# A two-layer graph network on one core: segments that begin at other row blocks, a tail of 12 column blocks in two passes of six, 64-column matmul pairs, and VectorE scaling the last output groups

## The reference, cut to what matters

```python
def layer0(X, adj, W, b):
    deg = clip(sum(adj, axis=1) + 1.0, 1.0)
    h = (adj @ X + X) / deg
    z = relu(concat([X, h], 1) @ W + b)
    return z / max(norm(z, axis=1), 1e-12)
def layer1(features, adj, W):
    neigh = adj @ features / (sum(adj, axis=1) + 1.0)
    return concat([features, neigh], -1) @ W.T
x = layernorm(x + layer0(x, adj, W0, b0))
x = layernorm(x + layer1(x, adj, W1))
```

## Time and profile before

| | us |
|---|---|
| median of three runs | 778.35 |
| the profiled execution's own time | 778.61 |
| its span, first to last instruction | 776.7 |
| PE busy (matmuls) | 662.5 (85%) |
| DVE busy | 710.8 (92%) |
| ACT busy | 619.5 (80%) |
| POOL busy | 211.1 (27%) |

### The profile page before, as it was taken

How to read it: one execution, slowest core, us unless ns; L and a number is a source line. 1 busy time by engine, 2 the same in 40 slices (tenths; PEclk the granted TensorE clock), 3 DMA queues, 4 the chain that set the end, 5 groups by cost and what they waited for, 6 DMA issues and landing times.

```text
span 776.7 us, 28012 instructions
## 1 busy us (share of the span) xinstructions
PE 662.5 (85%) x11173; PEld 610.1 (79%) x11173; DVE 710.8 (92%) x2703; ACT 619.5 (80%) x848; POOL 211.1 (27%) x302
## 2 busy tenths in 40 slices
PE   1457777878788888989899999999999999999992
PEld 0357677878677787878798989989998989988992
DVE  4699988999999999999999999999999999988894
ACT  4879798999989898989898988887888988840037
POOL 2225433535333332424313030211102020201024
PEclk9978897989999999999999999999999999999997
DMA  9999999999999999999999999999999999800004
GB/s 302 386 420 420 416 410 420 420 419 419 417 420 421 402 420 404 418 416 415 413 402 418 381 420 372 400 360 408 381 398 386 395 383 387 349 2 3 3 21 93
DMA packets 46125, 274.55 MB, mean 353 GB/s; under 512 B 12647, under 2 KB 12711, under 8 KB 13223
## 3 DMA queue, kind: packets, MB, share of 16 engines
q1 hardware_dynamic: 45184, 270.55, 87.0%
q0 software_dynamic: 576, 2.10, 0.8%
q10 hardware_dynamic: 230, 0.07, 0.0%
HBM read 270.60 MB, written 2.10 MB: 351 GB/s over the span
## 4 chain that ended last, share of the span: by engine, by line
DVE 31%; PE 27%; DMA 12%; issue 12%; ACT 10%; POOL 7%; ACTq 0%; DVEq 0%; SPq 0%; POOLq 0%
PE s_ps L367 13%; DMA a_in<-in_adj 9%; DVE e L766 9%; ACT junk L557 7%; DVE t_sb L773 6%; POOL small L1119 6%; PE u_ps L385 4%; PE p_ps L353 3%; DMA xl<-in_x 3%; DVE q_sb L839 2%; DVE y_sb L833 2%; DVE u_sb L773 2%; DVE a_in L773 1%; PE z_ps L431 1%; PE p_ps L442 1%
## 5 line engine op out<-in xcount | busy, mean ns | idle before, releaser
L557 ACT ACTIVATE junk<-a_in 128x2048 uint8<-128x2048 uint16 x256 | 489.6, 1919 | 3.1 <-DMA a_in<-in_adj 3.0
L367 PE MATMUL s_ps<-xh,t_sb 128*128 128x129 f16 x4096 | 377.9, 247 | 22.9 <-DVE t_sb L773 20.2
L367 PEld LDWEIGHTS s_ps<-xh,t_sb 128*128 128x128 fp8e4 x4096 | 306.2, 100 | 50.5 <-DVE t_sb L773 24.7
L766 DVE TENSOR_SCALAR e<-a_in 128x2048 fp8e4<-128x2048 f32 x256 | 310.7, 1224 | 7.8 <-DMA a_in<-in_adj 6.9
L1127 POOL COPY store<-pk 128x32 uint32<-128x32 uint32 (+1 forms) x250 | 130.2, 562 | 312.0 <-ACT pk L566 312.0
L353 PE MATMUL p_ps<-pow_bf,e 128*128 128x16 bf16 x4096 | 141.8, 170 | 62.7 <-DVE e L766 58.9
L353 PEld LDWEIGHTS p_ps<-pow_bf,e 128*128 128x128 fp8e4 x4096 | 128.9, 96 | 79.2 <-DVE e L766 72.9
L773 DVE TENSOR_SCALAR t_sb<-pk 128x128 uint32<-128x128 uint32 x1024 | 150.8, 222 | 5.3 <-ACT pk L566 4.8
L1119 POOL TENSOR_TENSOR small<-small,minus_half 128x4 f32<-128x4 f32 x32 | 74.6, 2332 | 203.9 <-DVE small L827 162.5
L385 PE MATMUL u_ps<-xh,u_sb 128*128 128x128 f16 x1488 | 99.2, 218 | 0.0
L385 PEld LDWEIGHTS u_ps<-xh,u_sb 128*128 128x128 fp8e4 x1488 | 88.9, 97 | 1.2
(11 more groups left out here) (110 smaller groups left out, 486.9 us busy)
## 6 DMA issues: line engine op xcount, KB each, us to landing
a_in<-in_adj SPq DMA_DIRECT2D x256, 1024.0 KB, 10.3
xl<-in_x POOLq DMA_DIRECT2D x4, 512.0 KB, 16.1
out_h<-e SPq DMA_DIRECT2D x8, 256.0 KB, 2.6
b_sb<-in_L_gnn_b ACTq DMA_DIRECT2D x3, 0.2 KB
w_sb<-in_L_gnn_W ACTq DMA_DIRECT2D x1, 32.0 KB
w_raw<-in_L_gnn_W ACTq DMA_DIRECT2D x1, 32.0 KB
```

Of the source, the lines that this page charges most:

```text
L367: last = nc.tensor.matmul(s_ps[:, n % 2, at:GW], t_sb[:, b, :], xh[:, b, at:GW], start=(b == 0), stop=False)
L557: nc.scalar.activation(junk[:, t % 2, :], halves[t % R], ACT.Copy, scale=1.0 / 128, accum_out=half_sum[:, n, c:c + 1]).then_inc(s_half, 1)
L766: nc.vector.tensor_scalar(e8[:, c, :], a_in[:, t % R, :], 1.0, None, ALU.is_equal, saturate=False).then_inc(s_e, 1)
```

## The change

`START` becomes 0, 12, 20, 28, 32, 40, 48, 56. `low` is then 0, 8, 16, 24, 28, 36, 44, 52; the segment from 32 has a catch-up width of four blocks (24 to 27, done in slots 32 to 39) and the others eight. TAIL is 52, and the 12 blocks left go in two passes of six (`TW`).

The 64-column pairs: `catch_up`, and `tail_sums` in the second pass, multiply the high part and the low part by two matmuls of 64 columns that add up in the same 64 columns of PSUM, in place of one matmul of 128 columns. `add_piece`, and `add_tail` in the second pass, then add once and not twice.

Outputs: ACT scales groups 0 to 3, DVE scales groups 4 to 7 (`scale_rows`, one instruction for eight rows), and DVE makes the squares of the last group itself (`last_variance`). SyncE waits on a second semaphore for groups 4 to 7. The tail has eight unpack buffers instead of six.

```diff
-START = [0, 12, 20, 28, 36, 44, 52]
+START = [0, 12, 20, 28, 32, 40, 48, 56]
-VR = 6
+VR = 8
+NA = 4
+WIDTH = [low(s + 1) - low(s) for s in range(NQ - 1)] + [NB - TAIL]
+TW = WIDTH[-1] // 2
 # catch_up, PE
-                    for b in range(W):
-                        last = nc.tensor.matmul(u_rows[:, r, :], u_sb[:, r * W + b, :],
-                                                xh[:, low(q - 1) + b, 0:HP], start=(b == 0), stop=(b == W - 1))
+                    for b in range(w):
+                        for part in range(2):
+                            last = nc.tensor.matmul(u_rows[:, r, 0:F], u_sb[:, r * w + b, :],
+                                                    xh[:, low(q - 1) + b, part * F:(part + 1) * F],
+                                                    start=(b + part == 0), stop=(b + part == w))
 # add_piece, DVE
-                link(nc.vector.tensor_tensor(rows, u_rows[:, 0:r1 - r0, 0:F], rows, ALU.add))
-                nc.vector.tensor_tensor(rows, u_rows[:, 0:r1 - r0, F:HP], rows, ALU.add).then_inc(s_uadd, 1)
+                nc.vector.tensor_tensor(rows, u_rows[:, 0:r1 - r0, 0:F], rows, ALU.add).then_inc(s_uadd, 1)
 # before the tail, PE
+            pe.wait_ge(s_glo, (TAIL + TW + BR - 1) // BR)
 # ACT, the end
-            for g in range(NV + 1):
-                if g < NV:
-                    squares(g)
-                if g:
+            for g in range(NV - 1):
+                squares(g)
+                if 1 <= g <= NA:
                     finish(g - 1)
 # DVE, new
+            def last_variance():
+                rows = slice(NB - TG, NB)
+                dve.wait_ge(s_vadd, 2 * NV)
+                dve.wait_ge(s_fvar, NV - 4)
+                for n in range(NB - TG, NB):
+                    ins = nc.vector.scalar_tensor_tensor(out=sqf[:, (NV - 1) % 4, n % TG, :], in0=acc[:, n, :], scalar=1.0,
+                                                         in1=acc[:, n, :], op0=ALU.mult, op1=ALU.mult,
+                                                         accum_out=fvar[:, 1, n:n + 1])
+                link(ins)
+                nc.vector.scalar_tensor_tensor(out=fvar[:, 1, rows], in0=fvar[:, 1, rows], scalar=1.0 / F,
+                                               in1=fvar[:, 0, rows], op0=ALU.mult, op1=ALU.add).then_inc(s_fvar, 1)
+            def scale_rows(g):
+                rows = slice(g * TG, (g + 1) * TG)
+                dve.wait_ge(s_froot, g + 1)
+                dve.wait_ge(s_out[g % 4], 16)
+                nc.vector.tensor_tensor(o_sb[:, g % 4, :, :], acc[:, rows, :], bc(fvar[:, 1, rows], TG),
+                                        ALU.mult).then_inc(s_o_dve, 1)
 # DVE, the end
             for g in range(NV):
+                if g >= 4:
+                    variance(g - 1)
+                if g >= NA + 2:
+                    scale_rows(g - 2)
                 add_tail(NV + g)
-                if g + 12 < 2 * NV:
+                if g < 4:
                     unpack_tail(g + 12)
-                if g:
+                if 1 <= g < 4:
                     variance(g - 1)
-            variance(NV - 1)
+            last_variance()
+            scale_rows(NV - 2)
+            scale_rows(NV - 1)
```

More of the change, by code:

```diff
@@ L75, in piece @@
     return j * ROWS[q - 1] // steps, (j + 1) * ROWS[q - 1] // steps
-PIECE = max(piece(n)[1] - piece(n)[0] for n in range(START[1], NB))
+PIECE = max((piece(n)[1] - piece(n)[0]) * WIDTH[seg(n) - 1] for n in range(START[1], NB))
 def turn(slot):
@@ L131, in gnn_kernel @@
         store = sb("store", [P, BASE[NQ]], U32)
-        u_sb = sb("u_sb", [P, PIECE * W, P], FP8)
+        u_sb = sb("u_sb", [P, PIECE, P], FP8)
         xh = sb("xh", [P, NB, GW + 1], F16)
@@ L232, in gnn_kernel @@
         s_o = sem("s_o")
+        s_o_dve = sem("s_o_dve")
         s_out = [sem(f"s_out{i}") for i in range(4)]
@@ L321, in _ @@
             for g in range(NV):
-                sp.wait_ge(s_o, g + 1)
+                if g < NA:
+                    sp.wait_ge(s_o, g + 1)
+                else:
+                    sp.wait_ge(s_o_dve, g - NA + 1)
                 sp.dma_start(out_g[g, :, :, :], o_sb[:, g % 4, :, :]).then_inc(s_out[g % 4], 16)
@@ L373, in sum_quarter, with catch_up @@
                     last.then_inc(s_sum, 1)
-            def catch_up(n, part):
+            def catch_up(n, half_of):
                 q, (r0, r1) = seg(n), piece(n)
-                if part == 0:
+                if half_of == 0:
                     pe.wait_ge(s_u, turn(n) + 1)
@@ L381, in catch_up @@
                         pe.wait_ge(s_uadd, turn(n))
-                half = (r1 - r0 + 1) // 2
-                for r in (range(half), range(half, r1 - r0))[part]:
-                    for b in range(W):
-                        last = nc.tensor.matmul(u_rows[:, r, :], u_sb[:, r * W + b, :],
-                                                xh[:, low(q - 1) + b, 0:HP], start=(b == 0), stop=(b == W - 1))
+                half, w = (r1 - r0 + 1) // 2, WIDTH[q - 1]
+                for r in (range(half), range(half, r1 - r0))[half_of]:
+                    for b in range(w):
[3 more added lines that the diff above has]
+                                                    start=(b + part == 0), stop=(b + part == w))
                     if r == r1 - r0 - 1:
@@ L438, in tail_sums @@
                     pe.wait_ge(s_vadd, j - 2)
-                at = TAIL + (j // NV) * W
+                at = TAIL + (j // NV) * TW
                 for r in range(TG):
-                    for b in range(W):
-                        last = nc.tensor.matmul(v_ps[j % 3][:, r, :], v_sb[:, j % VR, r * W + b, :],
-                                                xh[:, at + b, 0:HP], start=(b == 0), stop=(b == W - 1))
+                    for b in range(TW):
+                        if j < NV:
+                            last = nc.tensor.matmul(v_ps[j % 3][:, r, :], v_sb[:, j % VR, r * TW + b, :],
+                                                    xh[:, at + b, 0:HP], start=(b == 0), stop=(b == TW - 1))
+                            continue
+                        for part in range(2):
+                            last = nc.tensor.matmul(v_ps[j % 3][:, r, 0:F], v_sb[:, j % VR, r * TW + b, :],
+                                                    xh[:, at + b, part * F:(part + 1) * F],
+                                                    start=(b + part == 0), stop=(b + part == TW))
                 last.then_inc(s_vps, 1)
@@ L791, in unpack_piece @@
                     dve.wait_ge(s_ups, turn(n))
-                dst = words(u_sb[:, 0:(r1 - r0) * W, :])
+                dst = words(u_sb[:, 0:(r1 - r0) * WIDTH[q - 1], :])
                 unpack_planes(lambda g: dst[:, :, g * PKW:(g + 1) * PKW],
@@ L890, in unpack_tail @@
                 unpack_planes(lambda t: dst[:, :, :, t * PKW:(t + 1) * PKW],
-                              src[:, :, i * W:(i + 1) * W, :]).then_inc(s_v, 1)
+                              src[:, :, i * TW:(i + 1) * TW, :]).then_inc(s_v, 1)
             def add_tail(j):
@@ L898, in add_tail @@
                 rows = acc[:, (j % NV) * TG:(j % NV + 1) * TG, :]
-                link(nc.vector.tensor_tensor(rows, v_ps[j % 3][:, :, 0:F], rows, ALU.add))
-                nc.vector.tensor_tensor(rows, v_ps[j % 3][:, :, F:HP], rows, ALU.add).then_inc(s_vadd, 1)
+                ins = nc.vector.tensor_tensor(rows, v_ps[j % 3][:, :, 0:F], rows, ALU.add)
+                if j < NV:
+                    link(ins)
+                    ins = nc.vector.tensor_tensor(rows, v_ps[j % 3][:, :, F:HP], rows, ALU.add)
+                ins.then_inc(s_vadd, 1)
             def variance(g):
```

4 lines of the change are left out of this document (removed).

## The result

The changed kernel takes 787.38 us (median of 4 runs, 785.75 to 787.93), the kernel before 778.62 (4 runs on the same chip): a ratio of 1.0108, interval 1.0091 to 1.0126. It is 1.1% slower, where 0.2% faster was forecast. The profiled execution took 785.75 us, span 783.9, against 778.61 and 776.7 before. Single executions of the kernel before lay between 778.1 and 781.3 us in one session, so a microsecond between two profiles says little. The profiled execution is also the shortest of the four of the changed kernel; the other three took 787.3 to 787.9.

The account below looks back on a forecast made before the run. DVE was taken to set the pace from slot 20, with PE as full from slot 44. Stream +8.4, tail -6.1 and -4.0, clock +0.7 gave -1.0 us against 778.61: 777.6, median 777.3; range 771.5 to 783.

Parts of the forecast that it names:

- DVE sets the pace: Stream from slot 20 on: epochs of 41.0 to 42.7 us, DVE busy for all but 0.8 to 2.2 us.
- slots 28 to 31: Stream, eight blocks caught up in four slots: PE 42.2, DVE 41.2, so an epoch of 42.8 us, +1.8.
- slots 20 to 27: Stream, two epochs with DVE work 1.4 us less each: taken as -1.0 us each, -2.0 in all.
- slots 32 to 39: Stream, both engines below the loads' pace: epochs of 40.2 us against 41.5 and 42.1, -3.2 us.
- slots 40 to 47: Stream, PE 41.4 us and some 0.6 of stall: epochs of 42.0 us, -0.7 and -1.5.
- slot 48 to the first tail matmul: End of stream, PE-bound: +1.5, +1.9 and +10.8 us, last sums +0.2, less 0.4 for PE's lag at slot 48.
- tail, without the clock term: Tail: -6.1 us up to the end of `verdict`, where DVE becomes the bound, and -4.0 us after it.
- clock term: Tail: after PE idles 3.4 us its clock may fall to half speed; +0.7 us taken, bounds 0 and 1.7.
- rival A: Late slots dearer: 64-column matmuls in the PE-bound last 16 slots at 32 ns, not 29; 784 us, chance 0.16.
- Rival C: Catch-up pairs: a 64-column matmul costs the 16-column one's 25.6 ns; 770.8 us, chance 0.04.
- Rival D: Tail gives half: waits between three engines add up to more, 5 us less gain; 782.3 us, chance 0.10.
- POOL: Stream up to slot 31: 43 more copies (293 for 250) at 562 ns each cost nothing, nor slow DVE.

Follow-up runs that it names:

- run 1: Kernel before, with the first of the two DVE adds per piece left out in slots 12 to 35; ratio 0.9974 to the kernel before.
- run 5: Changed kernel with the old START table, two passes of eight and six unpack buffers, keeping 64-column pairs and DVE scaling; 773.36 us, ratio 0.9919.
- run 2: Changed kernel, with the catch-up of slots 28 to 31 done by 128-column matmuls and two adds; ratio 1.0051 to the kernel before.
- runs 10 to 12: run 5's kernel with DVE scaling groups 2 to 7; all eight; all eight, each before its group's variance; medians 773.4, 773.5, 773.4 us.
- run 9: Changed kernel, with the 16 packing matmuls of the second chunk of slot 3 issued five times; 784.73 us in one run.
- run 3: Changed kernel, with 128-column matmuls and two adds per piece in the whole stream, tail as changed; ratio 1.0077 to the kernel before.
- run 4: Changed kernel with START 0, 12, 16, 24, 32, 40, 48, 56, so the short segment stands at slot 12; ratio 1.0053 to the kernel before.
- run 6: Kernel before, with only DVE's scaling of groups 4 to 7, its last variance and the new end order; 781.43 us, ratio 1.0025.
- run 8: run 7's kernel, with 64-column pairs and one add in the second pass of the tail; ratio 0.9995 to the kernel before.
- run 7: run 6's kernel with segments of four slots and four blocks up to slot 36; ratio 1.0044 to the kernel before.

## Why the prediction was wrong

The step that failed first is "DVE sets the pace" from slot 20 on; the second is the sum for slots 28 to 31. By the prediction's own steps, in us, against the two profiled executions:

| step | forecast | measured |
|---|---|---|
| slots 20 to 27 | -2.0 | +0.1 |
| slots 28 to 31 | +1.8 | +6.0 |
| slots 32 to 39 | -3.2 | -4.7 |
| slots 40 to 47 | -2.2 | -0.9 |
| slot 48 to the first tail matmul | +14.0 | +16.4 |
| tail, without the clock term | -10.1 | -9.7 |
| clock term | +0.7 | 0 (1.7 to 2.7 in four other profiles) |

The stream up to slot 47 was to give 5.6 and gave nothing: PE began slot 48 at 517.8 us for 517.5. That is 6 of the 8 us by which the forecast missed the profiled execution (785.75 for 777.6). The median was missed by 10 (787.38 for 777.3).

*"From slot 20 on ... DVE sets the pace."* This step failed. Rows 1 show DVE busy for 39.48 of 41.70 us, and I took the idle 2.2 as something the edit wouldn't touch. In good part it was the waits for loads, 2.1 us over slots 20 to 27, and the same rows have the DMA share at 1.01 up to slot 39. An engine that is 95% busy beside a resource at its full share need not be the bound. Runs 1 and 5 and the waits after show the relief going into those waits. It isn't worth nothing everywhere: with the same program up to there, the profiles of runs 2, 5 and 10 to 12 reach slot 28 at 303.2 to 303.4 us, where the changed kernel has 304.8, run 9 304.5 and the kernel before 304.7. So slots up to 27 gave between 0 and 1.5 us for the 2.0 forecast. The faster epochs of slots 32 to 39 only made up for part of what slots 28 to 31 had lost, since loads had run ahead: at the start of slot 32 they were 4.9 chunks ahead of `compare`, for 3.9 before.

*"Slots 28 to 31: PE 42.2, DVE 41.2, so 42.8."* The work was right (42.81 and 41.44 busy). What failed is the step from work to time: 3.6 us of stops in which PE waits for its instructions, which I hadn't thought of, and up to 1.1 us of DVE waiting for PE and 3.7 for ACT. Behind the third stop PE's granted clock was also at 0.51 for 3.4 us from 350.1. Even without the long ones eight blocks in four slots cost 44.4 to 45.1 (runs 2 and 3, there through DVE), and spread out they cost 40.9 (run 4).

*Slots 48 to 63.* The mechanism was right, PE alone is the bound and its pairs are paid. The term that was mis-sized is the pair: 60.0 ns and not 58. On 816 pairs this is 1.6 of the 2.4 us missing. The rest is open; it isn't the pair, since run 3, with 128-column pairs, is also about 1 us over what the same sum gives for it. This is rival A, whose point of decision was 30.1 ns: the measured 30.0 is just at it, so that A by itself would have left the change within 0.2% of nothing. Rival C, 25.6 ns, and with it the table's 25 ns of the Trainium skill (TensorE: Matmul & The Clock Gate, Back-to-back issue gap), is excluded; the formula's 29.2 is near, and low by 0.8 ns.

*The tail* was right in both halves, and its chain as foreseen: waits for squares of 1.85, 0.98, 1.25 and 0.70 are 4.8 us for 4.5, the last root 1.53. Rival D (half the gain) didn't occur.

*The clock.* In the profiled execution it stayed at 1.00 over the first tail window though PE idled 3.08 us, so the term was 0. That was luck. Runs 2, 3, 4 and 9 have the same program in the tail and the same idle time, and in all four the clock was at 0.50 when PE began again, for 3.4 us in three and 6.8 in run 9. Run 4 is an example, PE's idle time (3.08 us, up to the transposes) and the window from where the clock fell, columns as in the earlier trace rows:

```profile
727.28 0.90 PE L430 MATMUL c_ps<-ident,h_sb 128*64 128x128 f32 x4 [3.08 <-DVE h_sb L863]
...
727.50:730.90 3.40, 3.40 (x32) 3.28 (x31) 3.37 (x16) 0.58 (x1) 0.00 (x0) 0.50 0.00 0
```

Their tails took 70.6, 70.5, 70.3 and 71.4 us for 68.7: 1.7 to 2.7 more, where the prediction had 1.7 as its upper bound. The three executions of the changed kernel that weren't profiled were 1.6 to 2.2 us longer than the profiled one, at a mean clock of 0.946 to 0.949 for 0.954. The same term would explain it, but where their clock fell isn't on record.

*POOL.* The copies were to cost nothing. They became longer, 782 ns in the mean for 562, but DVE's `compare` stayed at 1223 ns, the time the rows of before have (1.22), so nothing shows that they cost DVE anything. The long ones are those that run beside a `compare`: in the changed kernel 76 such copies took 2.40 us in the mean and the other 217 took 0.22. (A long copy is also more likely to meet one.)

*The balance.* The forecast weighed 1.8 and 14.0 in the stream against 10.1 in the tail and 5.6 of relief. The relief was the only thing that could pay for the table, and little of it was there. By the runs, the table costs 1.9% (run 5 against the changed kernel). With the old table, pairs in the stream bring the first tail matmul 3.9 us forward (695.4 for 699.4 in run 6, where profiles differ by 1), and pairs in the second pass make the tail 4.5 us shorter (run 8 against 7); the scaling alone costs 0.25%, 2 us (run 6). The last three add up to -6.4 us, and run 5 is 6.2 faster than the kernel before.

## What to carry to other kernels

Before a lighter engine is put down as time, look at what ends its idle moments: if the few it has are waits for a transfer at its full share, relief buys little. Moving work from a stage where two engines take turns to one where a single engine is full costs its whole price there (19.8 us for 7.4 here); replacing one instruction by two cheap ones is best where the other engine is the bound, and it can turn the bound round, as in the last groups of runs 10 to 12. Many short instructions beside saturated loads can have a price of their own that no engine's busy time shows. And a term that one profile shows at nothing, as the clock in the tail, can be there in most executions: compare it over all the traces with the same stage.
